# A transformer block with routed experts: second layer norm, routing and weight split placed inside the shared FFN stage, slot map by one-hot matmuls

## What is computed

```
x = x + cross_attention(layernorm(x), ctx)         # 16 heads of 16, biases, softmax over 64 keys
h = layernorm(x)                                    # second layer norm
shared = (silu(h @ sh_gate.T) * (h @ sh_up.T)) @ sh_down.T        # hidden width 512
p = softmax(h @ gate_w.T); w, idx = top_k(p, 2); w = w / sum(w)   # 8 experts
routed = sum over the two picks of w * ((silu(h @ eg[e].T) * (h @ eu[e].T)) @ ed[e].T)
out = x + shared + routed
```

## Time and profile before

| | us |
|---|---|
| median of 3 runs | 893.1 (890.27 to 895.41) |
| the profiled execution | 890.57 |
| its span | 888.7 |
| PE busy | 677.7 (76%) |
| DVE busy | 458.6 (52%) |
| ACT busy | 370.4 (42%) |
| POOL busy | 361.3 (41%) |

### The profile page before, as it was taken

The page is one execution under the profiler, slowest core; times in us unless marked ns, Lnnn a source line. Parts: engine busy times, 40 slices in busy tenths (PEclk is TensorE's granted clock), DMA queues, the critical chain, the costliest instruction groups (busy, mean ns, idle before and its releaser), DMA issues.

```text
span 888.7 us, 16489 instructions
## 1 busy us (share of the span) xinstructions
PE 677.7 (76%) x5030; PEld 393.2 (44%) x5031; DVE 458.6 (52%) x933; ACT 370.4 (42%) x583; POOL 361.3 (41%) x355
## 2 busy tenths in 40 slices
PE   3486676688887401078788789999999999999775
PEld 1232232345444300034444446666666666666433
DVE  2877785455656623645555524444444444444376
ACT  1144534656556324034333334444444444455311
POOL 3145454566675200077770134444444444443100
PEclk9977778555667655579999999999999999999998
DMA  6920000011111176344333033433333333333196
GB/s 205 71 60 1 0 0 0 1 37 26 37 31 31 37 154 163 85 122 111 104 97 118 18 84 91 91 90 83 95 90 92 91 88 91 88 94 75 65 306 227
DMA packets 130976, 74.40 MB, mean 84 GB/s; under 512 B 101298, under 2 KB 122868, under 8 KB 130932
## 3 DMA queue, kind: packets, MB, share of 16 engines
q1 hardware_dynamic: 121972, 54.79, 28.0%
q0 software_dynamic: 8960, 19.02, 7.2%
HBM read 37.84 MB, written 18.10 MB: 63 GB/s over the span
## 4 chain that ended last, share of the span: by engine, by line
PE 59%; DVE 13%; issue 10%; SPq 7%; ACT 5%; DMA 4%; POOL 2%; ACTq 0%; DVEq 0%; POOLq 0%
PE bank L1116 54%; SPq L421 5%; PE bank L1365 4%; DVE bank L837 3%; DVE arena L787 2%; PE bank L1171 1%; POOL map_d L555 1%; DMA arena<-y_d 1%; ACT arena L609 1%; DVE arena L881 1%; DMA arena<-arena 1%; DVE x_sb L874 1%; DVE hidden L1043 1%; ACT arena L682 1%; ACT arena L616 1%
## 5 line engine op out<-in xcount | busy, mean ns | idle before, releaser
L1116 PE MATMUL bank<-arena,w_stage 128*128 x1728 | 294.4, 327 | 10.4 <-issue 10.4
L1116 PEld LDWEIGHTS bank<-arena,w_stage 128*128 128x128 f16 x1728 | 167.0, 98 | 122.6 <-issue 14.5
L1116 PE MATMUL bank<-arena 128*128 128x34 f16 (+5 forms) x1220 | 151.0, 281 | 43.2 <-DVE bank L837 20.4
L575 POOL DMA_INDIRECT y_d<-w_stage,map_sb x72 | 71.3, 990 | 156.6 <-DVE w_stage L1077 98.8
L1116 PEld LDWEIGHTS bank<-arena 128*128 128x128 f16 (+2 forms) x1220 | 75.9, 115 | 114.6 <-DVE bank L837 40.1
L555 POOL DMA_INDIRECT map_d<-slot_row,pos_i x64 | 67.8, 1060 | 102.0 <-DVE slot_e L1016 82.8
L733 ACT COPY w_stage<-bank 128x1024 f16<-128x1024 f16 x72 | 72.9, 1012 | 83.8 <-PE bank L1365 83.5
L1083 DVE TENSOR_TENSOR hidden<-hidden 128x512 f16<-128x512 f32 x72 | 49.9, 692 | 105.0 <-ACT hidden L739 105.0
L1116 PE MATMUL bank<-qx,w_sh 128*128 (+1 forms) x384 | 93.6, 400 | 13.0 <-DVE w_sh L1021 12.4
L569 POOL DMA_INDIRECT w_stage<-rows_d,map_sb x72 | 70.1, 973 | 75.0 <-issue 60.6
L545 POOL TENSOR_TENSOR arena<-arena 128x512 f16<-128x512 f32 x64 | 72.5, 1155 | 53.0 <-ACT arena L642 36.7
(11 more groups left out here) (146 smaller groups left out, 749.6 us busy)
## 6 DMA issues: line engine op xcount, KB each, us to landing
w_stage<-in_w_all SPq DMA_DIRECT2D x27, 512.0 KB, 4.2
arena<-y_d SPq DMA_DIRECT2D x16, 512.0 KB, 5.7
x_sb<-in_x SPq DMA_DIRECT2D x8, 512.0 KB, 4.2
rows_d<-arena SPq DMA_DIRECT2D x8, 512.0 KB, 3.5
out<-x_sb SPq DMA_DIRECT2D x8, 512.0 KB, 3.7
map_sb<-map_d SPq DMA_DIRECT2D x72, 2.0 KB, 1.7
w_stage<-rows_d,map_sb POOLq DMA_INDIRECT x72, 2.8
w_stage<-w_stage SPq DMA_TRANSPOSE x72, 2.4
```

Of the source, the lines that this page charges most:

```text
L575: pool.indirect_dma_start(out=y_d, out_offset=bass.IndirectOffsetOnAxis(ap=map_sb[:, m, 1:2], axis=0), in_=y_sb[:, r], in_offset=None).the ...
L1116: return pe.matmul(o, a, b, start=first, stop=last, skip_group_check=not check)
```

## The change

- The second layer norm runs wholly on ACT for all four tiles, in the steps that `LN2_STEP` names (groups 0 and 1 before the first step). The `x2_hl` buffers are four deep. `gate(g)` stands in PE's stream at step `GATE_STEP[g]`.
- The six shared groups are unrolled, and `up(k)` runs ahead of `down(k - 1)` across groups. They use the banks 4 and 5 alone.
- The low halves of the weight pieces are shared by DVE (even pieces) and POOL (odd pieces, 128 x 1024). Three pieces are split in attention (units 4, 6, 8), twelve in steps 2 to 13, twelve in steps 19 to 23. SP's loads stand between the last transposes of attention and between those of the layer norm groups.
- Routing runs on DVE in steps 11, 13 and 14. The map is no longer scattered to HBM: in steps 14 to 17 DVE writes one-hot rows (`one_hot`), PE multiplies them (64 matmuls of 144 columns, `fill_map`), and in step 18 DVE reads the map from PSUM into `map_i`.
- The slots gather and scatter with `map_i`; DVE copies a slot's result unscaled, and `finish` multiplies by the weights (four tiles, two operations each). `xg` and `xgt` lie in `qx`. POOL's slot loop is unrolled, and its first gathers wait for the last `up` of the stage.

The core of the diff (lines left out are marked):

```diff
+        xg = qx[:, 0, 0, 0:4 * 2 * C].rearrange("p (r n) -> p r n", r=4)
+        xgt = qx[:, 0, 1, 0:4 * 2 * C].rearrange("p (r k t) -> p r k t", r=4, k=2 * HF)
...
-        map_d = nc.dram_tensor("map_d", (NS * P, 4), I32, kind="Internal").ap()
-        y_d = nc.dram_tensor("y_d", (TOP * T + NS * P, C), F32, kind="Internal").ap()
+        y_d = nc.dram_tensor("y_d", (NS * P + TOP * T, C), F32, kind="Internal").ap()
...
+        used[0] = 12 * 2048
+        hot_lane = carve([PICKS, P], F16)
+        hot_tile = carve([PICKS, 2, NS], F16)
...
+        GATE_STEP = (0, 2, 3, 5, 6, 7, 9, 10)
+        LN2_STEP = {0: 2, 1: 3, 3: 4, 4: 5, 6: 6, 7: 7}
+        SPLITS = {k: (k - 2, k - 1) for k in range(2, 14)} | {
+            19: (12, 14), 20: (14, 16), 21: (16, 19), 22: (19, 22), 23: (22, 24)}
...
-            for q in range(3):
+            for q in range(4):
...
+                if v >= NU - 3:
+                    load_w(v + 7 - NU)
...
+            for g in range(NG):
+                transpose_x2(g)
+                if g >= 2:
+                    store_x2(g - 2)
+                    load_w(g + 5)
+            store_x2(NG - 2)
+            store_x2(NG - 1)
+            for q in range(NG + 5, 3 * (E + 1)):
...
+            for q in range(1, 3 * (E + 1), 2):
+                w = w_sh[:, q] if q < 3 else w_qs[:, q - 3]
+                pool.wait_ge(w_hi, q + 1)
+                pool.tensor_tensor(w[:, 1], w_stage[:, q % 4, :], w[:, 0], ALU.subtract).then_inc(w_lo[q % 4], 1)
...
-            for t in range(NT):
-                for k in range(TOP):
-                    pool.indirect_dma_start(
-                        out=map_d, out_offset=bass.IndirectOffsetOnAxis(ap=pos_i[:, k, t:t + 1], axis=0),
-                        in_=slot_row[:, t, k, :], in_offset=None).then_inc(map_stored, 16)
...
+            pool.wait_ge(gu_ready, FSB)
...
+            for i in range(4):
+                gather(i)
+            for i in range(NS):
+                if i + 4 < NS:
+                    gather(i + 4)
+                if i >= 2:
+                    scatter(i - 2)
+            for i in range(NS - 2, NS):
...
+                for i in range(GT):
                     t = GT * g + i
                     ins = act.activation(x2[:, g % 2, i], x_sb[:, t, :], ACT.Identity,
                                          scale=rstd2[:, t:t + 1], bias=shift2[:, t:t + 1])
-                ins.then_inc(x2a_ready, 1)
...
+            def shared_step(k):
+                hc = k % FC
+                act.wait_ge(gu_ready, k + 1)
+                if k >= 2:
+                    act.wait_ge(hf_ready, k - 1)
+                act.activation(act_g[:, hc % 2], bank[hc % 2][:, :], ACT.Silu).then_inc(silu_ready, 1)
+                if k in LN2_STEP:
+                    norm2(LN2_STEP[k])
+                if k == 12:
+                    act.wait_ge(route_in, 1)
+                    act.activation(w2[:, :], w2[:, :], ACT.Exp).then_inc(route_exp, 1)
+                if k == 19:
+                    act.wait_ge(place_ready, 1)
+                for w in splits_of(k):
+                    split_hi(w + 3)
+                act.wait_ge(hf_ready, k + 1)
+                if k >= 2:
+                    act.wait_ge(down_used, k - 1)
+                act.copy(h_h[:, hc % 2], h_f[:, hc % 2]).then_inc(hh_ready, 1)
...
+                if u in (4, 6, 8):
+                    split_hi(u // 2 - 2)
...
+            def one_hot(c):
+
+                n = PICKS // 4
+                at = slice(n * c, n * (c + 1))
+                link3(dve.tensor_tensor(hot_tile[:, at, 1], slot_iota[:, :].unsqueeze(1).to_broadcast([P, n, NS]),
+                                        pick_tile[:, at].unsqueeze(2).to_broadcast([P, n, NS]), ALU.is_equal))
+                link3(dve.tensor_tensor(hot_tile[:, at, 0], hot_tile[:, at, 1],
+                                        pick_no[:, at].unsqueeze(2).to_broadcast([P, n, NS]), ALU.mult))
+                link3(dve.tensor_scalar(hot_tile[:, at, 1], hot_tile[:, at, 1], lane_no[:, 0:1], None, ALU.mult))
+                dve.tensor_tensor(hot_lane[:, at], lane_iota[:, :].unsqueeze(1).to_broadcast([P, n, P]),
+                                  pick_lane[:, at].unsqueeze(2).to_broadcast([P, n, P]),
+                                  ALU.is_equal).then_inc(hot_ready, 1)
...
+            def shared_step(k, between=None):
+                n, hc = divmod(k, FC)
+                dve.wait_ge(silu_ready, k + 1)
+                if k >= 2:
+                    dve.wait_ge(hl_ready, k - 1)
+                dve.tensor_tensor(h_f[:, hc % 2], bank[2 + hc % 2][:, :], act_g[:, hc % 2],
+                                  ALU.mult).then_inc(hf_ready, 1)
+                if hc == 0 and n not in (0, NGB):
+                    add_shared(n - 1)
+                if k - 1 in LN2_STEP:
+                    low_half(LN2_STEP[k - 1])
+                for g in range(NG):
+                    if k == GATE_STEP[g] + 1:
+                        take_logits(g)
+                if k == 11:
+                    best_two()
+                if k == 13:
+                    weights()
+                    places_in_expert()
+                if k == 14:
+                    places()
+                    for r in range(XB):
+                        dve.wait_ge(x2_stored[r], 16 * (NG // XB))
+                    one_hot(0)
+                if k == 15:
+                    one_hot(1)
+                if k == 16:
+                    one_hot(2)
+                if k == 17:
+                    one_hot(3)
+                    experts_of_slots()
+                if k == 18:
+                    read_map()
+                for w in splits_of(k):
+                    split_lo(w + 3)
+                dve.wait_ge(hh_ready, k + 1)
+                if k >= 2:
+                    dve.wait_ge(down_used, k - 1)
+                dve.tensor_tensor(h_l[:, hc % 2], h_f[:, hc % 2], h_h[:, hc % 2],
+                                  ALU.subtract).then_inc(hl_ready, 1)
+                if between is not None:
+                    between()
+
+            def add_shared(n):
...
+            def add_shared(n):
+                dve.wait_ge(down_used, FC * (n + 1))
+                for i in range(GT // 2):
+                    xt = x_sb[:, GT * n + 2 * i:GT * n + 2 * i + 2, :]
+                    ins = dve.tensor_tensor(xt, xt, bank[4 + i][:, :].rearrange("p (t c) -> p t c", t=2), ALU.add)
+                ins.then_inc(ffn_added, 1)
...
-                dve.tensor_tensor(xv, xv, yd[:, g % 2, 0], ALU.add).then_inc(yd_link, 1)
+                for t in range(GT):
+                    n = GT * g + t
+                    ins = dve.scalar_tensor_tensor(out=xv[:, t], in0=yd[:, g % 2, 0, t], scalar=w1[:, n:n + 1],
+                                                   in1=xv[:, t], op0=ALU.mult, op1=ALU.add)
...
+            for r in range(3):
+                pe.wait_ge(w_lo[r], 1)
+            gate(0)
+            up(0)
+            for k in range(1, FSB):
+                up(k)
+                for g in range(1, NG):
+                    if k == GATE_STEP[g]:
+                        gate(g)
+                if k == 12:
+                    count()
+                if 15 <= k < 19:
+                    fill_map(k - 15)
+                down(k - 1)
+            down(FSB - 1)
+
+
+            weights_split(pe)
```

More of the change, by code:

```diff
@@ L45, in build @@
     NGB = 6
+    PICKS = TOP * NT
+    FS = FC * NG
+    FSB = FC * NGB
     RT = 4
+    XB = 4
     OW = 2 * D + 2
@@ L269, in build @@
         x2l_ready = sem("x2l_ready")
-        x2t_got = [sem("x2t_got0"), sem("x2t_got1")]
+        x2t_got = [sem(f"x2t_got{i}") for i in range(XB)]
         lg_ready = sem("lg_ready")
@@ L276, in build @@
         w_hi = sem("w_hi")
-        w_lo = sem("w_lo")
+        w_lo = [sem(f"w_lo{i}") for i in range(4)]
         gu_ready = sem("gu_ready")
@@ L579, in _, with gather @@
-            run_slots(pool, slot)
+            for r in range(XB):
+                pool.wait_ge(x2_stored[r], 16 * (NG // XB))
+            pool.wait_ge(gu_ready, FSB)
+            def gather(i):
+                r = i % 4
+                if i >= 4:
+                    pool.wait_ge(xt_got[r], 16 * (i // 4))
+                pool.indirect_dma_start(
+                    out=xg[:, r], out_offset=None, in_=rows_d,
+                    in_offset=bass.IndirectOffsetOnAxis(ap=map_i[:, 0, i:i + 1], axis=0)).then_inc(x_got[r], 16)
@@ L679, in split_hi @@
-            def split_hi(w, q, turn):
-                act.wait_ge(w_loaded[q], 16 * turn)
-                act.copy(w, w_stage[:, q, :]).then_inc(w_hi, 1)
-            for q in range(3):
-                split_hi(w_sh[:, q, 0, :], q, 1)
-            act.wait_ge(route_in, 1)
-            act.activation(w2[:, :], w2[:, :], ACT.Exp).then_inc(route_exp, 1)
-            act.wait_ge(lg_copied, NG)
-            for r in range(2):
-                act.wait_ge(x2_stored[r], 16 * (NG // 2))
-                act.wait_ge(x2t_got[r], 16 * GT * (NG // 2))
```

(26 more changed lines are left out.)

413 lines of the change are left out of this document (180 added, 233 removed).

## The result

| | before | after |
|---|---|---|
| median of four runs, us | 892.0 (890.3 to 895.4) | 867.1 (866.8 to 868.2) |
| ratio | | 0.973 (0.970 to 0.976) |
| span of the profiled execution | 888.7 | 866.5 |

A forecast was written before the change was run, and what follows sets the result against it. PE bounds the routed slots; between attention and the shared FFN the core waits, with SP the pace until routing. Terms -60.7 + 41.7 - 0.7 + 1.7 = -18.0 take the span from 888.7 to 870.7, the median to 875.1 (854 to 892).

The forecast's parts named there:

- Attention, +2.4: End of attention: `load_w(5)` on SP waits for POOL's split of piece 1, so the last transposes go 2.4 us later.
- Start of the stage, 320.7: The first shared up matmul starts at 320.7 instead of 381.38, 60.7 us earlier.
- Length of the stage, 169.2: The shared stage, with the moved work in its 24 steps, takes 169.2 us instead of 127.5: +41.7.
- The port: Shared stage: DVE operations with two SBUF inputs are held up beside POOL's splits, some 8 us over the stage.
- Handover, -0.7: From the last `down` to the first slot matmul: 3.9 us where it is 4.6 now, -0.7.
- Slots, 0: Routed slots, 323.7 us: PE's instructions all stay, other changes lie beside a PE 98% busy, so 0.
- End, +1.7 (0.4 to 7): Last stage: `finish` becomes eight operations on 256 elements for two on 1024, +1.7 us (0.4 to 7).
- (a) Port and clock cost nothing: Shared stage: DVE's subtractions run beside POOL's and PE keeps its clock; 16 us fall away, 859; chance 0.28.
- (b) SP holds the pace: Six `load_w` between the groups' transposes hold SP 2.7 us each; 16 us, 891, no change; chance 0.08.
- (c) PE stays at 1.2 GHz: Shared stage: PE at half its full clock, +20, +12 and +14 over the steps, 921; chance 0.11.
- turning point: The loss of all 18 us takes a shared stage over 187 us, or slots that start after 511.8.
- The signs: Expected in the trace: SP gap at `load_w(7)`, ACT idle in step 4 for a store, DVE nearly full in steps 14 to 17.

## Why the prediction was right, and where its terms were off

The gain of the span, 22.2, comes out near the 18.0 in part by errors that cancel: the stage is 10.9 shorter than forecast, and start, handover, slots and end cost 2.7, 1.0, 0.5 and 2.5 more than forecast. Another 2.5 of the 24.9 is that the medians lie further apart than the two profiled executions. The mechanism holds: the waiting is gone, DVE sets the pace of steps 11 to 18, and the clock stays high.

- **Attention, +2.4:** the wait is right, the size too small. The statistics are ready at 311.86, 4.9 later than before; of that SP's wait is 2.1, and moving the loads gave 2.5. In one pair of traces the rest is within what two executions of one kernel differ by up to here (4.3); by the means above the loads cost 4.2 there and what else attention carries 1.5.
- **Start of the stage, 320.7:** measured 323.36, the 2.5 us that the statistics came later than forecast.
- **Length of the stage, 169.2:** measured 158.3, 10.9 less, the one large miss. Steps 0 to 10 have their `down` over 58.6 us from 332.31 to 390.92 (forecast 59.6), steps 11 to 18 over 52.4 us (58.4), 19 to 23 over 21.1 (21.8), and the way from 390.92 to 401.03 is 10.1 (10.4). The first `down` starts 9.0 after the first up, not 11.9: the table load of 1.28 runs while ACT is idle, and was costed on the path. The other 1.6 have no term: with half of the 7.93 for one up, the terms that I listed give 10.4, not 11.9. Steps 11 to 18 give 6.0: the one-hot block is right at 5.5, but of the seven intervals between these starts six are 0.6 to 1.4 shorter than I wrote, and one 0.3 longer. I had added 1.7 for slow matmuls after idle times of PE. They did come, around step 13 for example, where full speed is 1.47 and 2.75:

```profile
415.05 2.74 PE L1203 MATMUL bank<-w_sh,hidden 128*128 128x256 f16 x12 [4.42 <-DVE hidden L1122]
417.58 2.98 PE L1203 MATMUL bank<-qx,w_sh 128*128 128x512 f16 x12
```

But this up runs beside DVE's routing and block, which go from 414.31 to 424.86 without a pause, so that its slowness costs nothing there. How much of the 6.0 that explains isn't shown. Two readings were wrong, with little effect: a step of 3.90 is 24 matmuls and not 36, and the map's 16 take 1.16 to 1.18 at full speed and 1.65 and 2.10 after a wait, for the 1.7 forecast; and a copy of 512 at 0.28 gives 0.63 for 1152 in proportion, not 0.46, where 0.52 was measured.
- **The port:** confirmed by row and by run. Eight DVE operations of two SBUF inputs took 2.20 to 2.62 us beside POOL's splits in place of 0.68 or 1.22, 11.7 us more in all where I had taken 8; two more took 1.72 and 1.84 for 1.22. Not all of it is on the path: without POOL, and with 16 us more of work on DVE, 3.8 are gained. The Trainium skill (SBUF — State Buffer, "SBUF: two separate sides") says that of a DVE operation with two SBUF inputs and a GpSimd operation that reads SBUF the first to start has the port pair for its whole instruction, and the other is blocked. The trace agrees both ways: 2.62 for 0.68 on DVE, and POOL's split of 339.70, begun beside a DVE operation, takes 2.83 for 2.12.
- **Handover, -0.7:** +0.3. POOL's last split ends 3.2 us before the last `down`, as forecast (3.3), but from there to the first slot matmul are 8.1 us, not 7.15: the first gather took POOL 1.90, not 0.99, which is 0.9 of the 1.0.
- **Slots, 0:** +0.5.
- **End, +1.7 (0.4 to 7):** +4.2. I took four fused operations of 256 at the 1.38 of four single ones; they take 1.67, so a group is 3.34 for 2.46, +0.9. And it is paid more often than I had it: steps with a `finish` take 5.3 us where they took 4.4 when no load was waited for, and from the last `down` to the end are 12.9 us, where 11.0 were.
- **(a) Port and clock cost nothing:** false as a mechanism, since meetings are there; yet the time, 867.1, lies as near to its 859 as to 875, so the time alone doesn't decide between them. **(b) SP holds the pace:** false. Among the norm's transposes SP waits for a split once, 2.8 us at `load_w(7)`; the other pieces are split by the time, and its other waits there, 30.1 us in five, are for DVE's low halves. **(c) PE stays at 1.2 GHz:** false. The granted clock is 0.90 in the stage. (Its price for steps 11 to 18, +12, doesn't follow from what is said there: 7.8 us a step gives 3.7 over my steps, 10.4 a step 15.) Its turning point, a stage of over 187 us, was reached, but for 0.2, by the kernel with the old order at group ends: 186.8 us, 898.9 in all, 7.9 slower than before, and at a clock of 0.84. It got there by waits at the group ends, of DVE and then of PE, with slower matmuls behind them.
- **The signs:** ACT waits for a store in step 4, 1.65 us at 351.60, and SP at `load_w(7)`, as foretold; DVE is nearly full in steps 14 to 17.
- What I had not seen is how the gain divides. I wrote the order of `up(k + 1)` into the sum as one clause of the stage; alone it gives 16.4 us, and it is the condition for the rest.

## What to carry over

Before work is put under a stage, run its step order alone: an engine that works in order also holds back all that is queued behind its wait, so an order that was a small loss (3.3 us a group's end) becomes a large one (5.9) once the engine that waits is the busy one. When the busy engine gets help from another, look at what the helper holds: POOL's splits cost more in blocked DVE operations than they saved, and ACT's share of the one-hot work only moved the wait. Price each piece that moves in: here the pieces other than the norm cost 17.0 us net. Small fused operations add up where they lie in each step of a tail.

## What the hardware showed that I had not expected

- Four scalar_tensor_tensor of 256 f32 elements in a row take 1.67 us on DVE, four tensor_scalar of that size 1.38, and one addition of 1024 takes 1.23; four scalings of 256 take ACT 1.70.
- A DVE operation of 0.68 us on two SBUF inputs that begins beside a POOL subtraction ends 0.55 us after it (five times here); one of 1.22 us ends 1.1 after it (twice). A DVE product of 0.69 with one of its inputs in PSUM isn't held:

```profile
400.60 2.37 POOL L584 TENSOR_TENSOR arena<-w_stage,arena 128x1024 f16<-128x1024 f32 x1 [11.79 <-ACT arena L669]
```
```profile
400.89 0.69 DVE L1089 TENSOR_TENSOR hidden<-bank,hidden 128x512 f32<-128x512 f32 x1
```

- ACT's table load of 1.28 us runs as soon as ACT is free, at 318.12, 9.3 us before the silu begins; so do the two around the Exp, at 395.64 and 402.25.
- 16 small ACT copies of 72 elements take 2.55 us, 0.16 each.
